# Another order of the load queue in layer 2's attention, and layer 3's attention weights loaded one stage later

## The reference, cut to what matters

```python
k = (y @ Wk + bk).reshape(b, kv_t, NUM_HEADS, HEAD_DIM)
v = (y @ Wv + bv).reshape(b, kv_t, NUM_HEADS, HEAD_DIM)
content = jnp.einsum('bthd,bThd->bhtT', q + r_w_bias, k)
rel = jnp.einsum('bthd,bThd->bhtT', q + r_r_bias, pe)
rel = _relative_shift(rel)
attn = (content + rel) * (1.0 / math.sqrt(HEAD_DIM))
attn = attn * mask - 10000000000.0 * (1.0 - mask)
p = jax.nn.softmax(attn, axis=-1)
out = jnp.einsum('bhtT,bThd->bthd', p, v).reshape(b, t, DMODEL)
return out @ Wo + bo
```

## Time and profile before

| | us |
|---|---|
| runs, median of 3 | 1832.0 |
| profiled execution, its own time | 1838.59 |
| span of the profile (first to last instruction) | 1836.4 |
| PE busy over the span | 1431.1 (78%) |
| VectorE busy | 1202.8 (66%) |
| ScalarE busy | 592.9 (32%) |
| GpSimd busy | 366.9 (20%) |

### The profile page before, as it was taken

How to read it: one execution, slowest core, us unless ns; L and a number is a source line. 1 busy time by engine, 2 the same in 40 slices (tenths; PEclk the granted TensorE clock), 3 DMA queues, 4 the chain that set the end, 5 groups by cost and what they waited for, 6 DMA issues and landing times. The chain is left out here.

```text
span 1836.4 us, 32252 instructions
## 1 busy us (share of the span) xinstructions
PE 1431.1 (78%) x9741; PEld 1195.3 (65%) x9741; DVE 1202.8 (66%) x3015; ACT 592.9 (32%) x1724; POOL 366.9 (20%) x523
## 2 busy tenths in 40 slices
PE   4767999999999984580623577888789899889998
PEld 2336888888888874470521256666568688778887
DVE  5885667666777764789596857777645366445554
ACT  2331211221221212240210146666523466533232
POOL 4760000000000001100003433444323111122221
PEclk9668999999999996595865569999989899989999
DMA  5541211211211215354526258788512222200000
GB/s 185 178 149 33 58 29 29 57 29 29 57 29 38 49 27 138 102 161 56 126 68 183 88 143 180 177 184 183 119 58 72 68 81 83 60 19 17 23 17 17
DMA packets 194667, 156.14 MB, mean 85 GB/s; under 512 B 18806, under 2 KB 184519, under 8 KB 192296
## 3 DMA queue, kind: packets, MB, share of 16 engines
q1 hardware_dynamic: 163636, 125.26, 27.5%
q10 hardware_dynamic: 30964, 30.08, 5.5%
HBM read 108.47 MB, written 45.76 MB: 84 GB/s over the span
## 5 line engine op out<-in xcount | busy, mean ns | idle before, releaser
L720 DVE TENSOR_TENSOR moa_oe<-moa_mask,moa_ogT 128x1024 fp32r<-128x1024 bf16 x128 | 155.4, 1225 | 36.4 <-PE moa_k_ps L93 33.3
L91 PE MATMUL moa_k_ps<-moa_w_out_hi,moa_oe 128*128 128x256 f32 x512 | 150.4, 294 | 13.6 <-DVE moa_oe L720 13.6
L92 PE MATMUL moa_k_ps<-moa_w_out_lo,moa_oe 128*128 128x256 f32 x512 | 144.1, 282 | 0.0
L93 PE MATMUL moa_k_ps<-moa_w_out_hi,moa_oe 128*128 128x256 f32 x512 | 143.7, 281 | 0.0
L2009 PE MATMUL L_b_ps<-L_v,L_pT 128*128 128x128 f32 x1024 | 131.2, 287 | 1.2 <-issue 1.2
L2009 PEld LDWEIGHTS L_b_ps<-L_v,L_pT 128*128 128x128 f32 x1024 | 124.8, 201 | 6.8 <-issue 6.6
L91 PEld LDWEIGHTS moa_k_ps<-moa_w_out_hi,moa_oe 128*128 128x128 f32 x512 | 97.1, 190 | 22.4 <-issue 16.8
L1666 POOL TENSOR_TENSOR L_att<-L_masked,L_mask_add 128x512 f32<-128x512 f32 x64 | 81.4, 1272 | 151.2 <-DVE L_masked L1738 151.2
L687 DVE COPY_PREDICATED moa_v_sel<-moa_onehot,moa_y_ps 128x512 f32<-128x512 int32 x112 | 82.3, 735 | 35.3 <-DVE moa_v_sel L687 29.7
L1068 PE MATMUL proj_kv_ps<-proj_cT,L_wk 128*128 128x128 f32 x256 | 37.7, 295 | 85.8 <-PEq L1147 64.8
L1999 PE MATMUL L_r_ps<-ident,L_prob 128*128 128x128 f32 x512 | 77.3, 283 | 32.7 <-DVE L_pT L1722 26.1
(11 more groups left out here) (341 smaller groups left out, 3830.5 us busy)
## 6 DMA issues: line engine op xcount, KB each, us to landing
bounce<-L_rel SPq DMA_DIRECT2D x64, 258.0 KB, 4.9
moa_mask<-chosen SPq DMA_DIRECT2D x32, 512.0 KB, 5.9
L_shifted<-bounce SPq DMA_DIRECT2D x64, 256.0 KB, 4.4
L_values<-proj_v ACTq DMA_DIRECT2D x32, 136.0 KB, 2.1
L_v<-L_values SPq DMA_DIRECT2D x32, 136.0 KB, 2.9
ret_staged_values<-in_w_value_dram ACTq DMA_DIRECT2D x8, 512.0 KB, 3.8
ret_staged_outputs<-in_w_out_dram ACTq DMA_DIRECT2D x8, 512.0 KB, 4.0
ret_cT<-in_ctxT_pairs_dram SPq DMA_DIRECT2D x16, 256.0 KB, 2.9
```

Source lines behind the costliest of these rows:

```text
L91: pe.matmul(out, x_hi, w_hi, start=first, stop=False)
L92: pe.matmul(out, x_hi, w_lo, start=False, stop=False)
L93: return pe.matmul(out, x_lo, w_hi, start=False, stop=last)
L720: dve.tensor_tensor(oe[e % 2][:, :, :, :].rearrange("p a m s -> p a (m s)"), mask[:, e, :, :].rearrange("p m s -> p (m s)").unsqueeze(1).t ...
```

## The change

Layer 2's SP list of step b becomes: x of b+4; keys of b+3, once keys of b+1 are consumed; mask of b+2, once the mask of b has been multiplied; store of the result of b-1 and residual of b+1; values of b+2, after `pv_done` of batch b; then the four writes of b+2, the wait for the last `add_relative` of b+1 and the four reads of b+2, as before. Layer 3's list stays as it was. The distances load layer 2's weights alone; layer 3's are issued by ACT in the warp, after the first two context loads, and the two bias products move from VectorE's head to GpSimd's end.

```diff
--- before.py
+++ after.py
@@ -965,8 +965,7 @@
 
             @block.scalar
             def _(act):
-                for w_later in later_weights:
-                    w_later.load(act)
+                later_weights.load(act)
 
                 def step(b, u, ahead=True, front=True, middle=True, tail=True):
                     nu = 1 - u
@@ -1046,11 +1045,11 @@
         pool.wait_ge(self.row_zeroed, after(1))
         pool.memset(self.first_row[0:1, :], 1.0).then_inc(self.setup, 1)
 
-    def biases(self, dve):
-        dve.wait_ge(self.weights[1].loaded, self.weights[1].LOADED)
+    def biases(self, pool):
+        pool.wait_ge(self.weights[1].loaded, self.weights[1].LOADED)
         for par in range(2):
-            dve.tensor_scalar(self.key_bias[:, par, :], self.weights[1].bk[:, :], self.k.pair_mask[:, par:par + 1], None,
-                              ALU.mult).then_inc(self.bias_set, 1)
+            pool.tensor_tensor(self.key_bias[:, par, :], self.weights[1].bk[:, :],
+                               self.k.pair_mask[:, par:par + 1].to_broadcast([128, DT]), ALU.mult).then_inc(self.bias_set, 1)
 
     def load(self, act, n, u):
         act.dma_start(self.cT[u][:, :, :], self.k.ins["ctxT_pairs"][n, 0].rearrange("(t p) s -> p t s", p=128)).then_inc(self.cT_loaded[u], 16)
@@ -1169,11 +1168,13 @@
                     pool.memset(zeros[:, :], 0.0).then_inc(zero_set, 1)
                     pool.memset(entry[:, :], 0.0).then_inc(zero_set, 1)
                     projection.constants(pool)
+                    projection.biases(pool)
 
                 @block.scalar
                 def _(act):
                     for n in range(2):
                         projection.load(act, n, n)
+                    context_weights[1].load(act)
                     for n in range(B // 2):
                         projection.store(act, n, n % 2)
 
@@ -1184,7 +1185,6 @@
 
                 @block.vector
                 def _(dve):
-                    projection.biases(dve)
                     dve.wait_ge(dist_in[0], after(16))
                     dve.wait_ge(big_set, after(2))
                     dve.wait_ge(zero_set, after(2))
@@ -1624,27 +1624,31 @@
                     if ahead and (not isinstance(b, int) or b + 4 < B):
                         sp.wait_ge(ln.xn_ready, after(b + 3))
                         load_x(b + 4, u)
+                    if relative and ahead and (not isinstance(b, int) or -2 < b < B - 3):
+                        sp.wait_ge(k_ready, after(b + 2))
+                        sp.wait_ge(k_ready_act, after(b + 2))
+                        load_keys(b + 3, nu)
+                    if relative and ahead and middle and (not isinstance(b, int) or b + 2 < B):
+                        sp.wait_ge(masked_ready, after(b * 4 + 4))
+                        load_mask(b + 2, u)
                     if tail:
                         sp.wait_ge(xo_ready, after(b))
                         sp.dma_start(x_out[b - 1], xo[nu][:, :]).then_inc(x_stored[nu], 16)
                         if not isinstance(b, int) or b + 1 < B:
                             load_residual(b + 1, nu)
-                    if ahead and (not isinstance(b, int) or b >= 0):
-                        if relative:
-                            sp.wait_ge(k_ready, after(b + 1))
-                            sp.wait_ge(k_ready_act, after(b + 1))
-                        else:
-                            sp.wait_ge(s_done, after(b * 4 + 4))
+                    if relative and ahead and (not isinstance(b, int) or b >= 0):
+                        sp.wait_ge(pv_done, after(b + 1))
+                        load_values(b + 2, u)
+                    if not relative and ahead and (not isinstance(b, int) or b >= 0):
+                        sp.wait_ge(s_done, after(b * 4 + 4))
                         load_keys(b + 2, u)
-                    if front and (not isinstance(b, int) or b >= 1):
+                    if not relative and front and (not isinstance(b, int) or b >= 1):
                         sp.wait_ge(pv_done, after(b))
                         load_values(b + 1, nu)
                     if ahead and relative:
                         for r in range(4):
                             write_group(b, u, r)
                         sp.wait_ge(att_ready, after(b * 4 + 8))
-                        if middle and (not isinstance(b, int) or b + 2 < B):
-                            load_mask(b + 2, u)
                         for r in range(4):
                             read_group(b, u, r)
 
@@ -2609,7 +2613,7 @@
         x, x_in = x_after(3), x
         dist, costs = scratch("dist", (B, S, S)), scratch("costs", (B, S + 1, S + 1))
         steps, path = scratch("steps", (B, S, S)), sb("path", [128, B * S])
-        stage_distances(k, x_in, dist, (L2_weights, L3_weights))
+        stage_distances(k, x_in, dist, L2_weights)
         k.clear_semaphores()
         held = lambda layer, *keys: ContextScratch(scratch(f"{layer}_keys", (B, 128, *keys)),
                                                    scratch(f"{layer}_values", (B, 128, 2, H // 2 * (HD + 1))))
```

## The result

The changed kernel takes 1843.3 us, the median of 7 runs (1836.2 to 1844.8), against 1828.8 for the kernel before in the same session (7 runs, 1828.1 to 1832.2): 1.0069 of it, 95% interval 1.0055 to 1.0084. Slower, where I had forecast 1825 and faster.

The account below looks back on a forecast made before the run. No engine fills layer 2's steps; the DRAM round trip was the root of mask and keys waits. Layer 2 -1.0 and distances -6.3 made -7.3 us: 1831.3 against the profiled execution, 1825 on the median, range 1803 to 1837.

Parts of the forecast that it names:

- 6.1: Layer 2: first write goes 6.1 us after the first addition of shifted scores, 0.6 later than before, behind the values' wait.
- its upper bound: Layer 2's round trip through DRAM: writes limited by what DRAM absorbs, so it stays 9.1 to 9.6 us; 9.3 taken.
- Rival B: Layer 2: packed writes run at the engines' rate, steps of 13 to 14.8 us, 1789 to 1814 in all; chance 0.25.
- the sum 6.1 + 9.3 + 0.1: Layer 2's new step: first write at 6.1, round trip 9.3, then 0.1: 15.5 us, before 0.1 for the half clock.
- about +3.5: Layer 2: keys three ahead by themselves would bring the first write to about +3.5 us after the addition, against +5.5.
- my 6.3: Head of the distances: without layer 3's eight DMAs on ACT the stage gains 6.3 us, bounds 5.2 and 6.8.
- rival D: Distances: x and context loads gate the first batches, 0 to 2 us gained, about 1831 in all; chance 0.10.
- hidden where I said: Warp: layer 3's first projection some microseconds late, hidden by PE's idle 64.8 us before the second half.
- the delay that I weighed: Distances' second piece: sharing DMA engines with the weights could double its time, a 1 us stall; nothing in the sum.
- I add 0.1 for it, taking it as rare and partly overlapped: Layer 2: PE's half clock after its wait, now on the loop, priced at 0.1 us a step, making 15.6.
- rival C: Layer 2: half clock lands on the loop, such steps take 17 us; 1836, or 1844 in every step; chance 0.15.
- -6.3 and -1.0: The two parts' forecast gains in us: layer 3's weights out of the distances -6.3, layer 2's queue -1.0.

Follow-up runs that it names:

- weights alone: Kernel before with only layer 3's weights loaded in the warp and the bias products on GpSimd, layer 2's queue old: 0.9963 of before.
- the variant with 0.8: Changed kernel with 24 matmuls repeated (groups 0, 1 and 0 weighed again) in PE's wait ahead of the first pair: 1.0011 of before.
- the two without a wait: Changed kernel with VectorE's copy of the fourth group ahead of the first addition, 0.9874 of before; the same plus values behind the writes, 0.9784.
- the old values' wait: Changed kernel with the values' load ahead of the writes but loading batch b+1 after the weighing of b-1, as before the change: 0.9865 of before.
- queue alone: Kernel before with only layer 2's new SP list, layer 3's weights staying where they were: 1.0119 of before.
- two other kernels: Kernel before with only the keys three batches ahead, 0.9952 of before; kernel before with only the mask at the head of SP's list, 1.0020.

## Why the prediction was wrong

**Right.** Keys' and mask's waits go, and their new waits at the head of SP's list cost nothing: SP is through with that head 3.3 us before the values may go. The first write follows the values' issue, and that the fourth weighing: +6.2 in a step with the full clock, where I had 6.1. Packing the writes buys next to nothing: the round trip is 9.29 on average, I took 9.3 from its upper bound, and on the one chip that ran both kernels it is 9.74 against 9.78 before. Rival B falls. With it falls the time by the Trainium skill ("DMA: Bandwidth & Descriptors", Anatomy of one DMA), whose fit for GpSimd's path, 2.0 us plus bytes at 436 GB/s, gave 7.0 for these DMAs of SP's queue. The three steps of the changed kernel with the full clock take 15.44, 15.34 and 15.77 us, a mean of 15.5: the sum 6.1 + 9.3 + 0.1.

Three smaller readings were off and carried nothing in the sum. The DMA share of 0.80 was not the highest column; PE's 167.25 of 203.60 us is 0.82. At 1181.50 three writes had still to land, not two; the second landed at 1181.97. And the first write that the keys alone would allow, put at about +3.5, measured 4.17.

**The distances.** 6.0 in the trace for my 6.3, and 0.9963 alone; rival D falls. The warp paid nothing that shows, by its row in the waits of 770 to 990 us and by the distances' second piece in the DMA view, answering to the earlier trace rows:

```profile
PE proj_kv_ps L1067 <- PEq L1146: 56.9, 1, 56.9
```

```profile
warpf_dd<-dist SPq DMA_DIRECT2D x1, 256.0 KB, 4.9
```

PE's wait ahead of the second half shrank from 64.8 to 56.9 us, so a later first half was hidden where I said. The piece landed 4.9 us after its issue, 5.3 before, so the delay that I weighed did not come. It had no occasion to: by the DMA view ACT's queue moved 0.26 MB between 771 and 776 us, as much as before the change, when it had the context alone to bring, and the 1.30 MB of the weights moved between 779 and 786, when the piece had landed. The Trainium skill's rule of turns between queues ("DMA: Bandwidth & Descriptors", Queues, rings and completion order) is neither borne out nor refuted by this.

**The step that failed** is one term: "I add 0.1 for it, taking it as rare and partly overlapped". The half clock was on the loop in 11 of 14 steps. Those take 17.2 on average against 15.5, 1.7 longer, so it cost 11/14 x 1.7 = 1.3 us a step where I had 0.1, and 14 x 1.2 = 17 us over the stage. That is rival C with its mechanism, its place and nearly its price (1.5; "in every step it would be 1844"); I gave it 0.15, and cut its slow end out of the range.

Two things misled me. I took the half clock as rare from the kernel before (one of the two steps shown, 0.94 in the mean). Even that was not what the rows gave: the trace has it in 4 of 14 steps (3.13, 3.21, 3.58 and 3.48 us for groups 0 and 1), and 4/14 x 1.5 = 0.4 a step is four times my term; the rest I took off as overlap, without a row for it. And I carried the count over with the wait. But PE's wait didn't only move, it grew. Before, it stood ahead of the transposes, 26.1 / 14 = 1.9 us a time, with others elsewhere in the step:

```profile
PE L_r_ps L1999 <- DVE L_pT L1722: 26.1, 14, 2.9
```

Now it stands in one place at 38.7 / 13 = 3.0 us. Over the changed kernel and its variants the slow steps go with this wait: 11 or 12 of 14 where it is 2.8 to 3.2 us on average over all steps, 3 to 6 where it is 1.4 to 1.5, none in the variant with 0.8 and in the two without a wait. A single wait doesn't decide it: with the old values' wait one of 2.30 us was followed by the full clock and one of 1.93 by the half. Nor does a slow step bring on the next: PE waited 2.97 us on average behind a slow step and 3.01 behind one at full clock, and in the two other profiles with most steps slow (queue alone, and changed on the other chip) it waited less behind slow ones (3.2 against 3.5, and 3.3 against 4.0). What makes one step slow and the next not stays open.

Before the change a slow weighing of groups 0 and 1 fell partly beside the keys' wait: with the old list (before, weights alone, before on the other chip) such steps were 0.2 to 0.5 us longer than the rest. In one step each of the latter two it reached groups 2 and 3 as well, and these took 17.9 and 17.3 us.

In the sum: I forecast -6.3 and -1.0; alone, the two parts measure -6.8 and +21.8 us (0.9963 and 1.0119 of 1836.4).

## What to carry to other kernels

A load moved ahead in a queue brings its wait with it: ask what stands behind that wait, and whether the engine that ends it waits, further round, for what stands behind it. If a change gathers an engine's idle time into one place on the loop, price the work just behind it at the half clock as the normal case, not as the exception; here it was 11 or 12 of 14 steps behind waits of about 3 us. The same change gave 1.4% with the load behind the urgent transfers and cost 0.7% with its wait ahead of them.

## What I had not expected of the hardware

The lower clock held also while no DMA ran beside PE. In the slowest step of the changed kernel PE waited 3.38 us; the pair then took 2.08 instead of 1.14 and the weighing 3.78, with the DMA engines idle for part of it (columns of the second fence as in rows 1; the share of the DMA engines is the one before the last):

```profile
1185.73 2.08 PE L1979 MATMUL L_r_ps<-L_pz,L_qrT 32*128 32x256 f32 x8 [3.38 <-DVE L_pT L1726]
1187.75 3.78 PE L2013 MATMUL L_b_ps<-L_v,L_pT 128*128 128x128 f32 x16
```

```profile
1189.00:1190.00 1.00, 1.00 (x6) 1.00 (x6) 0.02 (x1) 1.00 (x4) 0.00 (x0) 0.50 0.00 0
```

The round trip through DRAM differed with the chip: 9.29 and 9.74 us for the changed kernel in its two profiles, and 8.55 to 8.94, in two other kernels, on the one where the kernel before was fastest. Packing made no difference between the kernels before and changed on one chip (9.78 and 9.74); with the values behind the writes, and the hole back, it took 0.6 longer. On that fastest chip no step of the two kernels run there had a slow weighing; whether the change would lose there too was not tried.
